# Numbering the result rows of a routed feed-forward layer by partition first and block second

## The reference, cut to what matters

```
x = x + attention(cond(x, side))            # 16 heads, 4 key/value heads, causal
x = x + ffn(cond2(x, side))                 # mixture of experts

def ffn(h):                                  # h: 1024 tokens x 256
    probs = softmax(h @ gate_weight.T)       # 64 experts
    weight, expert = top_k(probs, 8)         # 8 experts ("picks") for each token
    weight = weight / weight.sum()
    for each token and each of its 8 picks:
        gate, up = split(h @ gate_up[expert])        # 256 -> 2 x 96
        y += weight * ((silu(gate) * up) @ down[expert])   # 96 -> 256
    return y
```

## Time and profile before

| what | value |
|---|---|
| median of 3 runs | 538.47 us (535.09, 538.47, 540.96) |
| span of the profiled execution, first to last instruction | 534.3 us |
| mean granted TensorE clock in it | 0.974 of full |
| TensorE busy (matmul) | 478.1 us, 89% |
| VectorE / ScalarE / GpSimd busy | 352.2 / 332.2 / 238.5 us |
| moved by DMA | 108.54 MB in 71560 packets, mean 203 GB/s |
| read back from `pair_d` | 16 reads of 512.0 KB |

### The profile page before, as it was taken

One profiled execution on the slowest core, in us unless ns is written; L12 is line 12 of the kernel. 1 busy time (PEld: TensorE's weight loads), 2 busy tenths in 40 slices (PEclk: granted clock), 3 DMA queues, 4 the chain that ended last, 5 costly groups with the idle time before them and its releaser, 6 DMA issues.

```text
span 534.3 us, 10363 instructions
## 1 busy us (share of the span) xinstructions
PE 478.1 (89%) x2751; PEld 388.2 (73%) x2751; DVE 352.2 (66%) x1175; ACT 332.2 (62%) x1021; POOL 238.5 (45%) x255
## 2 busy tenths in 40 slices
PE   3886999999989799999998647999999999999875
PEld 1466767887778777778875636889999898999621
DVE  5868488487398489479679744856666665666432
ACT  4556786888676879777987813555555555555400
POOL 0354102011012571101577777767667676765700
PEclk9899999999999999999999859999999999999989
DMA  7930992000030220300277246999999999993497
GB/s 274 421 130 20 301 334 85 1 1 1 2 80 10 73 76 10 76 2 0 82 269 275 91 150 187 368 400 399 400 393 388 397 396 398 385 366 131 150 354 250
DMA packets 71560, 108.54 MB, mean 203 GB/s; under 512 B 10234, under 2 KB 49351, under 8 KB 71120
## 3 DMA queue, kind: packets, MB, share of 16 engines
q1 hardware_dynamic: 62336, 90.93, 48.3%
q0 software_dynamic: 9168, 16.95, 8.7%
HBM read 81.31 MB, written 34.77 MB: 217 GB/s over the span
## 4 chain that ended last, share of the span: by engine, by line
PE 61%; DVE 14%; ACT 12%; DMA 6%; issue 4%; SPq 2%; POOL 1%; POOLq 0%; DVEq 0%; ACTq 0%
PE ps L1474 14%; PE ps L1214 10%; PE ps L1494 9%; PE ps L1339 7%; ACT lg L634 4%; DVE lg L912 3%; ACT lg L577 3%; PE ps L1262 2%; PE ps L1210 2%; PE ps L1212 2%; PE ps L1211 2%; PE ps L1255 2%; SPq L414 2%; PE ps L1320 2%; PE ps L1327 2%
## 5 line engine op out<-in xcount | busy, mean ns | idle before, releaser
L563 POOL DMA_INDIRECT pair_rows<-eout,dest x127 | 126.0, 992 | 54.9 <-DVE dest L1185 42.2
L1474 PE MATMUL ps<-wts,xg 128*128 128x192 f32 x508 | 105.0, 330 | 0.0
L1474 PEld LDWEIGHTS ps<-wts,xg 128*128 128x128 f32 x508 | 80.8, 193 | 0.1
L774 ACT ACTIVATE sact<-ps 128x96 f32<-128x96 f32 x127 | 31.9, 251 | 75.8 <-PE ps L1474 75.8
L1494 PE MATMUL ps<-wts,aT 96*128 96x256 f32 x254 | 76.0, 381 | 0.0
L1182 DVE COPY xg<-ps 128x256 f32<-128x256 f32 x127 | 53.9, 424 | 29.0 <-PE ps L1214 28.5
L634 ACT ACTIVATE lg<-lg,mneg 128x128 f32<-128x128 f32 (+1 forms) x128 | 56.4, 442 | 26.1 <-DVE mneg L912 26.1
L1195 DVE SCALAR_TENSOR_TENSOR aact<-sact,xrow,ps 128x96 f32<-128x96 f32 x127 | 39.9, 314 | 48.1 <-ACT sact L774 47.7
L483 POOL DMA_INDIRECT slot_rows<-rows,pair_slot x48 | 48.1, 1002 | 32.9 <-DVE hit L977 20.1
L577 ACT ACTIVATE eout<-ps 128x256 f32<-128x256 f32 x127 | 48.8, 384 | 17.2 <-PE ps L1494 1.2
L1214 PE MATMUL ps<-ident,xrow 128*128 128x128 f32 x254 | 50.1, 278 | 9.5 <-DMA xrow<-slot_rows 9.5
(11 more groups left out here) (220 smaller groups left out, 1043.3 us busy)
## 6 DMA issues: line engine op xcount, KB each, us to landing
wts<-in_experts_dram SPq DMA_DIRECT2D x127, 320.0 KB
xrow<-slot_rows SPq DMA_DIRECT2D x127, 130.0 KB, 7.9
slot_rows<-zero SPq DMA_DIRECT2D x1, 8320.0 KB, 28.3
pairs<-pair_rows SPq DMA_DIRECT2D x16, 512.0 KB
wT<-in_wq_t_dram SPq DMA_DIRECT2D x4, 512.0 KB, 6.8
wq_raw<-in_wq_l_dram SPq DMA_DIRECT2D x1, 2048.0 KB, 14.9
wo_sb<-in_wo_l_dram SPq DMA_DIRECT2D x1, 2048.0 KB, 20.7
bm<-bias_rows SPq DMA_DIRECT2D x4, 512.0 KB, 3.5
```

The costliest lines, as they stand in the source:

```text
L563: nc.gpsimd.indirect_dma_start(out=pair_d, out_offset=bass.IndirectOffsetOnAxis(ap=dest[:, t:t + 1], axis=0), in_=eout[t % NOUT][:], in_of ...
L1474: ins = nc.tensor.matmul(ps[:, 2 + u % 2, 0:I2], xg[u % 3][:, cc, :], wts[u % NBUF][:, cc * I2:(cc + 1) * I2], start=(cc == 0), stop=(cc = ...
```

## The change

The result row of a pair gets another id. Before, the row of partition p and block t within a pick was t x 128 + p; after, it is p x 8 + t. Two places write ids (the iota of `number_rows` and that of `number_last_rows`) and one place reads by them (L414). `dest`, the scatter, `slot_d`, the order of the expert tiles, the tile `pairs` and everything that reads it are as they were: `pairs[r]` at partition p and block b still holds the same pair's result.

```diff
                 for h in range(2):
                     sp.dma_start(pairs[r][:, h * HB:(h + 1) * HB],
-                                 pair_d[k * NT + h * HB * P:k * NT + (h + 1) * HB * P].rearrange("(b p) c -> p b c", p=P)
+                                 pair_d[k * NT:(k + 1) * NT].rearrange("(p b) c -> p b c", p=P)[:, h * HB:(h + 1) * HB]
                                  ).then_inc(wts_ld[2 * r + h], 16)
@@ number_rows
-                nc.gpsimd.iota(r[:, :, C + 1], pattern=[[NT, TOPK]], base=t * P, channel_multiplier=1,
+                nc.gpsimd.iota(r[:, :, C + 1], pattern=[[NT, TOPK]], base=t, channel_multiplier=NTB,
                                allow_small_or_imprecise_dtypes=True).then_inc(ids_set, 1)
```

## The result

The changed kernel takes 535.46 us (median of 20 runs, 533.40 to 538.95), the kernel before 538.32 us beside it (20 runs): ratio 0.9949, 95% interval 0.9925 to 0.9974. That is 2.9 us less, 1.4 to 4.0 by the interval. Two later comparisons of the same kernel gave 0.9957 (0.9930 to 0.9984) and 0.9954 (0.9924 to 0.9983).

What follows compares the result with a forecast made beforehand. DMA's rate on the final reads was taken to bound the end. Terms of -2.0, -0.8 and -0.3 us gave -3.1; 534.3 - 3.1 + 4.2 = 535.4 us, range 532.2 to 539.5.

Steps and rivals of the forecast that it cites:

- The bound: From 504 to 527 us the end is set by the rate of the DMA engines and nothing else.
- Iotas and scatter at 0: Id iotas and the 127 scatter issues cost the same; a 12 us DMA lull before 500 us covers slower writes: 0 us.
- 513 to 527 us, -2.0 us: Late reads alone: 4.88 MB at 406 GB/s instead of 348 take 12.0 us instead of 14.0.
- 504 to 513 us, -0.8 us: Early reads, last scatters mixed in: 3.34 MB at 406 GB/s take 8.2 us instead of 9.
- the start, -0.3 us: First reads, 500.7 to 504 us: fewer pieces to set up may shorten it, bounds 0 and -1.0 us.
- the slower rival: Bad stride: 4 KB reads with partitions 8 KB apart at L414 run at 295 GB/s, +4.8 us, 543.3 us; chance 0.08.
- The sum: All terms over the read phase together: -3.1 us.
- The 4.2 us added for what a run has beyond its span: Median run time lay 4.2 us above the profiled 534.3 us span; added to reach the forecast time.
- The gates at 0: Reads waiting for late scatters stay hidden behind queued reads; step 2's out at 506.9 us, last gate by 514.7: 0 us.
- The ceiling: Rival: device memory, not packet size, limits the late reads to 348 GB/s; nothing gained, 538.5 us; chance 0.20.
- The 6% for 4 KB over 1 KB: Estimate from the skill's fixed packet overhead: 131 beats against 140 for the reads, sum about -1.5 us.
- TensorE's lower clock: At 1.2 GHz TensorE's spare 0.6 us per step is gone; on the last step, the end is up to 2 us later.

Runs made afterwards that it cites:

- the run with 1 KB runs in the new numbering: Changed kernel with the two halves' blocks taking turns within a partition's 8 KB, so reads find 1 KB runs; ratio to the kernel before 1.0002.
- without holes: Changed kernel renumbered by half, partition, block: 4 KB runs, each half read one 512 KB stretch; ratios to before 0.9934, 0.9951. Whole-step reads also lack holes.
- the single gate: All 16 reads wait until every scatter has landed; ratios to before: kernel before 1.0169, changed kernel 1.0086, numbering by half, partition, block 1.0105.

## Why the prediction was right, step by step

- **The bound** is as said: DMA's rate sets the read phase, and TensorE and VectorE wait for it at each step. TensorE's steps were forecast 2.6 us apart, and the last four are 2.5 to 2.6 apart.
- **Iotas and scatter at 0**: the tile stretch is unchanged, and the run with 1 KB runs in the new numbering has the time of before.
- **513 to 527 us, -2.0 us** at 406 GB/s: the rate became 414, which is 14.0 - 4.88/0.414 = 2.2 us. This is the step that carries the gain. That it is the packet, the run with 1 KB runs shows.
- **504 to 513 us, -0.8 us, and the start, -0.3 us: wrong.** In the 12 us from the first issue the kernel before moved 12 x 316 = 3.79 MB; the changed one moved no more. Its windows below, from the three profiles of it:

```profile
500.46:512.46 12.00, 9.93 (x26) 4.29 (x24) 3.85 (x5) 2.43 (x9) 6.50 (x6) 0.86 0.92 311
```

```profile
503.33:515.33 12.00, 8.58 (x26) 3.83 (x24) 3.71 (x5) 2.44 (x9) 6.85 (x6) 1.00 0.93 307
```

```profile
501.00:513.00 12.00, 7.85 (x22) 3.89 (x21) 3.08 (x4) 2.38 (x9) 6.04 (x6) 0.87 0.84 280
```

I took for the early stretch the rate of the late one. What stands in its place is a slower first 4 us and the slow spell: 4 KB packets at 237 to 334 GB/s for 4 to 7 us. I had seen the like, 295 GB/s from 5.5 to 7 us, and used it only as the bound and as the slower rival. That rival was half right. It happens, for a part of the time, and eats the 1.1 us that I expected from the early stretch; without holes the first 12 us move 12 x 356 = 4.27 MB. What makes the spell is not shown.
- **The sum** of -3.1 us against 2.9 measured agrees better than its parts, and that is luck: of its terms, -2.0 held and -1.1 did not. The read time fell by 1.9, 1.7 and 1.6 us in the three profiles. So 1.0 to 1.3 us of the measured 2.9 have no place in the profiles. The interval (1.4 to 4.0 us) takes in 1.7, so it may be scatter of the runs; that stays open. The 4.2 us added for what a run has beyond its span were partly scatter too: the changed kernel's profiled run took 533.95 us with a span of 532.2, 1.8 us more, and the other profiled runs show the same.
- **The gates at 0**: right. Step 2's reads went out at 507.3 us, where I had 507. Step 1's, for which I had worked out nothing, went out at 504.1 us (the row below), 2.0 us later than before (502.1). By then DMA had moved some 0.6 MB, scatters included, of the 1.05 MB of step 0, so its reads were not used up. The last gate opened at 515.3 us, 0.6 us later than I worked out, behind 11 us of queued reads.

```profile
L414 SPq DMA_DIRECT2D pairs<-pair_rows x2: 320/377/434, 504.1 to 504.5; - x2
```

- **The ceiling** (0.20) is refuted by 387, 414 and 428 GB/s at 2, 4 and 8 KB. The 6% for 4 KB over 1 KB that follow from the Trainium skill's page "DMA: Bandwidth & Descriptors", section Why small descriptors are slow, are too few here: measured are 161 against 4 x 51.9 = 208 ns, 23% less.
- **TensorE's lower clock** fell between 507 and 512 us in the changed kernel (0.66 granted on average, 0.50 from 508 to 511). Eight matmuls took 5.49 us there, and the next step still waited 1.23 us for data, so it cost nothing.

## What to carry to other kernels

Where reads set the end and their pieces are small, lay the data out so that one partition's piece is long: here each packet cost, as estimated above, about 15 ns beside its 37 ns per KB, and going from 1 KB to 4 KB raised the late reading rate by 19% (348 to 414 GB/s). Don't carry the steady rate over to the first microseconds of a stream, and look whether a read leaves holes: the same 4 KB runs without holes moved 14% more in the first 12 us beside scatters (356 against 311 GB/s). Check such a gain with a control that changes the layout and keeps the piece, as the 1 KB runs did.

## What the runs showed that was not expected

- A packet of the same size has two costs: in the kernel before 375 GB/s in the mixed stretch against 348 alone, though its pieces stayed 1 KB. With the single gate, and no scatter near, the rate falls to 345 to 356 GB/s from the fifth microsecond on, when the read queue is full; beside scatters it stays at 352 to 400 GB/s for nine. So either the full queue slows the packets or the scatters mixed in raise the rate; no run separates the two.
- Slow spells of 4 KB packets (237 to 334 GB/s at a DMA share of 0.76 to 0.97, so in some the engines also stood idle in part) occur in all five runs that read 4 KB out of every 8. Of the five runs that read without holes, the four beside scatters have none, and the one with the single gate has a short one. The cause isn't shown.
- GpSimd's scatter issue of 0.98 us once took 1.57 us in the changed kernel and 1.92 us in its second profile, with reads in the queues. The last gate opened later by it, under 11 us of queued reads. Behind the reads a late scatter also lands later: 7.3 and 7.55 us after its issue in the kernel before and the changed one, against 2.3 us for the last one in each of the three runs with the single gate, where no read was queued.
